# Values and scores exchanged in TensorE's order of the cross-attention head loop of a two-layer Perceiver

## The reference, cut to what matters

```
scores = einsum('bhsr,bhlr->bhsl', q_r, k_r)          # 256 x 4096 a head
attn   = softmax(scores, axis=-1)
ctx_c  = einsum('bhsl,bld->bhsd', attn, kv_r)         # 256 x 128 a head
ctx_lat = einsum('bhsd,hkd->bhsk', ctx_c, w_kc_kv)
out    = ctx @ Wo.T                                   # summed over the heads
```

## Time and profile before

| | |
|---|---|
| median of 3 runs | 1218.99 us (1218.53 to 1219.9) |
| span of the profiled execution | 1220.0 us |
| PE busy | 1082.8 us (89%), 6491 instructions |
| DVE busy | 781.7 us (64%) |
| ACT busy | 549.0 us (45%) |
| POOL busy | 318.3 us (26%) |
| granted TensorE clock, mean | 0.919 |

### The profile page before, as it was taken

How to read it: one execution, slowest core, us unless ns; L and a number is a source line. 1 busy time by engine, 2 the same in 40 slices (tenths; PEclk the granted TensorE clock), 3 DMA queues, 4 the chain that set the end, 5 groups by cost and what they waited for, 6 DMA issues and landing times.

```text
span 1220.0 us, 18949 instructions
## 1 busy us (share of the span) xinstructions
PE 1082.8 (89%) x6491; PEld 904.4 (74%) x6492; DVE 781.7 (64%) x1285; ACT 549.0 (45%) x1073; POOL 318.3 (26%) x198
## 2 busy tenths in 40 slices
PE   5965977999999889989999999999999999888865
PEld 4843857888888766658888888888888888676832
DVE  2446425455555466668888888888888888553636
ACT  1510514334344232246555666565666556534322
POOL 5022003333443220003332222333333332312502
PEclk9567568999999999999999999999999999979987
DMA  8303004455455133251012223222122112223010
GB/s 252 96 18 156 1 2 136 174 220 208 182 185 190 48 104 107 77 196 26 12 29 39 38 37 37 37 37 32 34 34 33 28 26 38 41 78 142 1 56 17
DMA packets 72808, 97.72 MB, mean 80 GB/s; under 512 B 37664, under 2 KB 55232, under 8 KB 71616
## 3 DMA queue, kind: packets, MB, share of 16 engines
q1 hardware_dynamic: 72768, 97.18, 28.1%
HBM read 92.26 MB, written 4.90 MB: 80 GB/s over the span
## 4 chain that ended last, share of the span: by engine, by line
PE 58%; DVE 22%; issue 10%; ACT 4%; POOL 3%; DMA 1%; DVEq 0%; SPq 0%; POOLq 0%; ACTq 0%
PE PS L1346 11%; PE PS L1366 9%; PE PS L1356 6%; DVE hL L892 4%; PE PS L1253 3%; DVE qsL L942 3%; DVE pL L968 3%; DVE scores L948 3%; POOL hw L493 2%; PE PS L1295 2%; PE PS L1314 2%; PE PS L1166 2%; PE PS L1304 2%; PE PS L1178 2%; PE PS L1423 2%
## 5 line engine op out<-in xcount | busy, mean ns | idle before, releaser
L948 DVE TENSOR_SCALAR_CACHE_REDUCE scores<-PS 128x512 f32<-128x512 f32 x256 | 174.0, 689 | 89.3 <-PE PS L1346 87.6
L669 ACT ACTIVATE scores<-scores,nmX 128x512 f32<-128x512 f32 x256 | 181.9, 714 | 52.7 <-DVE nmX L952 52.1
L687 ACT ACTIVATE pH<-PS 128x1024 fp32r<-128x1024 f32 x128 | 131.0, 1023 | 154.1 <-PE PS L1356 154.1
L968 DVE TENSOR_TENSOR pL<-PS,pH 128x1024 fp32r<-128x1024 f32 x128 | 156.2, 1220 | 7.3 <-ACT pH L687 7.3
L1356 PE MATMUL PS<-ident,scores 128*128 128x128 f32 x1024 | 136.4, 274 | 17.8 <-ACT scores L669 16.0
L506 POOL TENSOR_TENSOR wrow<-wrow,winv 88x1024 f32<-88x1024 f32 x16 | 30.3, 1892 | 466.9 <-DVE winv L988 466.9
L1356 PEld LDWEIGHTS PS<-ident,scores 128*128 128x128 f32 x1024 | 115.9, 141 | 44.4 <-issue 33.6
L1366 PE MATMUL PS<-pH,kvH 128*128 128x256 f32 x512 | 146.7, 287 | 0.7 <-DVE pL L968 0.5
L1366 PE MATMUL PS<-pH,kvL 128*128 128x256 f32 x512 | 145.2, 284 | 0.0
L1366 PE MATMUL PS<-pL,kvH 128*128 128x256 f32 x512 | 144.7, 283 | 0.0
L1346 PE MATMUL PS<-kvTH,qsH 128*128 128x512 f32 x256 | 112.2, 438 | 1.5 <-DVE qsL L942 1.5
(11 more groups left out here) (294 smaller groups left out, 2417.8 us busy)
## 6 DMA issues: line engine op xcount, KB each, us to landing
rawG<-in_wg SPq DMA_DIRECT2D x16, 768.0 KB, 4.4
rawU<-in_wu SPq DMA_DIRECT2D x16, 768.0 KB, 5.9
rawD<-in_wd SPq DMA_DIRECT2D x16, 768.0 KB, 7.3
wrow<-in_w SPq DMA_DIRECT2D x16, 352.0 KB
win<-in_win SPq DMA_DIRECT2D x1, 4640.0 KB, 16.1
wblk<-blocks SPq DMA_DIRECT2D x4, 1056.0 KB, 9.6
wb<-w_rows SPq DMA_DIRECT2D x32, 128.0 KB, 3.2
wqX<-in_wqX SPq DMA_DIRECT2D x16, 256.0 KB, 2.6
```

Source lines behind the costliest of these rows:

```text
L669: act.activation(at, at, ACT.Exp, bias=nmX[:, b, q:q + 1], accum_out=csum[:, b, q, c:c + 1]).then_inc(exp_done, 1)
L687: act.activation(pH[:, c % 2], PS[:, 2 + 2 * (c % 2):4 + 2 * (c % 2), :].rearrange("p k (h t) -> p (k h) t", t=T), ACT.Copy).then_inc(pH_r ...
L948: dve.tensor_scalar(sp_[:, q, c * CH:(c + 1) * CH], PS[:, q, :], 1.0, None, ALU.mult, ALU.max, accum_out=cmax[:, q, c:c + 1]).then_inc(sX_ ...
L968: dve.tensor_tensor(pL[:, c % 2], PS[:, 2 + 2 * (c % 2):4 + 2 * (c % 2), :].rearrange("p k (h t) -> p (k h) t", t=T), pH[:, c % 2].bitcast ...
```

## The change

In `pe_scores`, inside the loop over chunks, `weigh(n, c - 1)` is issued ahead of `scores(n + 1, 1 - b, c)` instead of behind it:

```
                 for c in range(NCH):
                     if c:
                         turn(n, c)
+                    if c:
+                        weigh(n, c - 1)
                     if not last:
                         scores(n + 1, 1 - b, c)
-                    if c:
-                        weigh(n, c - 1)
                     if not (isinstance(n, int) and n == 0):
                         if c == 1:
                             values(n - 1, 1 - b, i + b)
```

## The result

| | before | after |
|---|---|---|
| median | 1219.45 us (1218.53 to 1221.94, 4 runs) | 1331.66 us (1329.3 to 1333.63, 4 runs) |
| ratio | | 1.0926, 95% interval 1.0911 to 1.0941 |
| profiled execution: time, span | 1221.94, 1220.0 us | 1333.63, 1331.8 us |
| PE busy | 1082.8 us (89%) | 1110.0 us (83%) |
| PE idle before matmuls of line 1366, released by line 968 | 0.5 us | 93.3 us |

The exchange costs 112 us, 9.3%. The forecast was 1327 us, within 1302 to 1354. One of the four runs of experiment 7 was slow (1766.62 us at a granted clock of 0.64, beside 0.92 in the others), and its median here is of the three others.

A forecast was written before the change was run, and what follows sets the result against it. PE was taken as the bound, with no slack. Chunks of 4.99 us instead of 3.69 made heads 40.41 us against 33.26; 1220.0 + 108.2 - 1.0 = 1327 us, range 1302 to 1354.

The forecast's parts named there:

- The wait: Middle of a head: weigh waits for pL behind DVE's evacuation of scores, starting 2.06 us after scores end; +1.30 a chunk.
- Rival O: PE's order in the follow-up runs: the order itself costs the 1.3 us a chunk; no chance given.
- The size: One chunk on PE: 2.06 wait, 1.54 weigh, 1.39 scores, 4.99 us instead of 3.69.
- The sum: Whole loop: seven chunks and one head's end, 40.41 us a head against 33.26; 1327 us, chance 0.80.
- nothing lies around the span: Profiled execution: its span of 1220.0 us was taken as 1.0 over the median, with nothing outside it.
- the signs: Profile after: PE busy about 80 in 100 us, idle before line 1366 about 1.2 us a chunk, heads 40.4 us apart.
- Line 942: DVE's query split after chunk 6: ends just after POOL's line 509, hidden with 0.47 us to spare before scores(7).
- The rival that it loses the gap: Line 942 waits for a further POOL operation, delaying scores(7) by 1.6 us in 14 heads: +23 us, 1350; chance 0.09.
- The clock: TensorE in each chunk: granted clock falls while PE does only transposes; 158 us on top, 1485; chance 0.07.
- The other side: Wait cheap, head's end pays: break-even if weigh starts within 1.04 us after scores; at best -23 us, 1196; chance 0.03.

The follow-up runs named there:

- experiment 7: Changed kernel with DVE computing pL for only 512 of each chunk's 1024 columns, the other half staying zero; 1274.11 us, ratio 1.0457 to the kernel before.
- Experiment 1: Changed kernel with DVE doing pL ahead of the evacuation of scores for chunks 0 to 6; 1225.39 us, ratio 1.0053 to the kernel before.
- experiment 2: Kernel before, old PE order, with only DVE's pL moved ahead of the evacuation of scores for chunks 0 to 6; 1226.74 us, ratio 1.0057.
- experiment 5: Kernel before with values and scores exchanged in chunk 2 of each head alone; 1217.74 us, ratio 1.0001.
- experiment 6: Kernel before with values and scores exchanged in chunk 1 of each head alone; 1238.24 us, ratio 1.0173.
- experiment 9: Changed kernel with the query split early (ACT after chunk 2, DVE's line 942 after chunk 3); 1330.74 us, ratio 1.0936 to the kernel before.
- experiment 8: Kernel before, old order, with the query split early (ACT after chunk 2, DVE's line 942 after chunk 3); 1197.63 us, ratio 0.9832.
- experiment 3: Kernel before with values and scores exchanged in chunks 1 and 3 of each head alone; 1238.77 us, ratio 1.0164.

## Why the prediction was right

*The wait.* The claim was that weigh(c-1) would catch up with pL, which stands on DVE behind the evacuation of scores(c-1). Experiment 1 removes that position alone and takes back 106 of 112 us, and its control, experiment 2, accounts for the rest. Experiments 5 and 6 place the wait: the same exchange costs nothing where another weigh lies between, and 1.35 us a head where none does. Experiment 7 shows the DVE instruction counting one for one. Rival O, that transposes followed by weigh's matmuls, their weight loads or the clock cost the time, is excluded by 1 and 5.

*The size.* From the end of scores to weigh 2.06 us were forecast and are 2.09; weigh was put at 1.54 and is 1.54, scores at 1.39 and is 1.39, the whole chunk at 4.99 and is 5.02. The 0.03 is on DVE, from its first bank to the end of pL: 758.56 - 756.02 = 2.54 instead of 2.51, most of it in the start of the second bank, 0.70 after the first (756.72 - 756.02) instead of 0.68 as in the earlier trace rows. At the head's end turn was put 1.37 after the end of scores(7) and comes at 783.00 - 781.60 = 1.40; weigh(7) was put at 2.55 and comes at 2.57.

*The sum.* From DVE's first start in head 0 (542.12) to the first turn of head 15 (1144.66) the forecast was 602.5 us. After:

```profile
543.14 0.69 DVE L948 TENSOR_SCALAR_CACHE_REDUCE scores<-PS 128x512 f32<-128x512 f32 x1 [2.28 <-PE PS L1346]
...
1148.45 0.63 PE L1356 MATMUL PS<-ident,scores 128*128 128x128 f32 x4 [0.43 <-ACT scores L669]
```

That is 605.3 us. Before, it was 1036.13 - 542.12 = 494.0, so the loop grew by 111.3 of the 112.2 us, 2.8 more than forecast, and 105 x 0.03 = 3.2 us accounts for them. Outside the loop two small things nearly cancel and are not explained: its start came 1.0 us later (543.14 beside 542.12), and what follows it is 0.5 us shorter. Of the signs, PE's busy share was put at about 80 and is 83.54, for the reason given under the table. The idle time before line 1366 was put at about 1.2 us a chunk and is 1.05, or 0.62 where `values` fills part of it. One bookkeeping step was loose: the prediction says that nothing lies around the span, and the profiled execution took 1.9 us more than its span (1221.94 beside 1220.0). The forecast started from the median, so this only hid that the profiled execution was the slowest of the four.

*Line 942.* It was to be hidden, with POOL's line 509 still setting its end:

```profile
774.90 0.17 DVE L988 RECIPROCAL winv<-wscale 88x3 f32<-88x3 f32 x1
...
778.43 1.88 POOL L509 TENSOR_TENSOR wrow<-wrow,rounding 88x1024 f32<-88x1024 f32 x1
...
779.20 1.40 DVE L942 TENSOR_TENSOR qsL<-qp,qsH 128x256 fp32r<-128x256 f32 x1
...
780.47 1.89 POOL L512 TENSOR_TENSOR wint<-wrow,rounding 88x1024 bf16<-88x1024 f32 x1 [0.16 <-POOL wrow L509]
```

It ends at 780.60, 5.53 us after line 988 (forecast 5.55), in the gap behind line 509, 0.51 us before DVE starts on scores(7) at 781.11. The rival that it loses the gap did not come, and experiment 9 shows the whole of its old cost gone. The Trainium skill (SBUF — State Buffer, "SBUF: two separate sides") says that a VectorE instruction with two SBUF inputs and a GpSimd one that reads SBUF exclude each other for a whole instruction. The rows agree on VectorE's side: line 942 lasts 1.40 us here and 0.42 in experiment 8 with GpSimd idle, and ends 0.29 after line 509 does (780.31).

*The clock.* It did not fall. At the end of head 0 PE did only eight transposes from the end of scores(7) at 578.77 to weigh(7) at 581.29, 2.5 us, and the clock stayed at 1.00. In the kernel before these were 3.1 us, and it fell to 0.54. The stretch of the changed kernel:

```profile
580.00:582.00 2.00, 1.75 (x14) 1.54 (x15) 1.34 (x3) 2.00 (x6) 1.97 (x1) 1.00 0.00 0
```

The Trainium skill (TensorE: Matmul & The Clock Gate, "A second HAM failure mode: psum-queue depth-cycling") tells of a kernel whose clock swung between its two levels because PE idled briefly and often between groups of matmuls. That did not happen here: in a round of 5.02 us PE had 2.09 between scores and weigh, up to 1.05 of them idle and the rest mostly transposes, and the granted clock stayed at 1.00 from 540 to 1140 us.

*The other side.* The break-even at 1.04 us from the end of scores to weigh was not put to the test by a kernel that has just that wait. That some gain lies at the head's end was right, and experiment 8 collects it (21 us) with no exchange.

## What to carry to other kernels

Before two pieces of work on a full engine are exchanged, write down for each what the other engine does between it and its consumer, in that engine's own order. Here the distance that mattered was not from turn to weigh but from scores to weigh, because the evacuation of scores stood ahead of pL. Work between a producer and its consumer's wait is cover. Here the need was 2.09 us. With 3.69 us of cover the wait was free, with 0.88 it cost 1.3 us in each of 105 chunks, and where an exchange left 2.22 us (chunk 3 of experiment 3) or 2.66 (experiment 5) it cost nothing.

And look which idle time hangs on a neighbour: moving one small VectorE operation, which took 2.57 us beside GpSimd, to where GpSimd rests was worth 21 us over the loop (together with its counterpart on ScalarE).

## What was not expected of the hardware

The price of VectorE's line 942, two SBUF inputs of 128x256, was known as 2.57 us beside GpSimd's work; moved to where GpSimd is idle it takes 0.42 us (experiments 8 and 9, median of 16). Nothing in the trace marks the difference as a wait. It shows as busy time of VectorE, so the busy share counts a stall as work.
